# A graph layer: the rows of one tile in every second batch come from one-hot products on PE instead of a gather

## The reference

```
h   = max(layernorm(x), 0)
ea  = edge_attr @ W_edge.T + b_edge
msg = relu(h[src] + ea)
agg = segment_sum(msg, dst)
out = x + relu(((1 + eps) * h + agg) @ W1.T + b1) @ W2.T + b2
```

## Time and profile before

| | |
|---|---|
| time, median of 3 runs | 1233.08 us |
| time of the profiled execution | 1224.89 us |
| its span, first to last instruction | 1223.1 us |
| POOL busy | 785.8 us (64%) |
| DVE busy | 607.6 us (50%) |
| ACT busy | 518.7 us (42%) |
| PE busy | 496.0 us (41%) |
| mean granted TensorE clock | 0.673 |

### The profile page before, as it was taken

The page is one execution under the profiler, slowest core; times in us unless marked ns, Lnnn a source line. Parts: engine busy times, 40 slices in busy tenths (PEclk is TensorE's granted clock), DMA queues, the critical chain, the costliest instruction groups (busy, mean ns, idle before and its releaser), DMA issues.

```text
span 1223.1 us, 7306 instructions
## 1 busy us (share of the span) xinstructions
PE 496.0 (41%) x1592; PEld 249.7 (20%) x1592; DVE 607.6 (50%) x739; ACT 518.7 (42%) x713; POOL 785.8 (64%) x838
## 2 busy tenths in 40 slices
PE   2143344344344334245343253442534334425358
PEld 2011111222121112012111121120211111112146
DVE  6665544555554445364536345352545363543563
ACT  5134444344433335353435333343535343433434
POOL 6766666666666666575757575766757575757530
PEclk9967766767767766566666665666656666666669
DMA  7523333222223223242323332322423232322212
GB/s 217 148 66 71 83 78 68 67 68 68 67 67 68 68 68 98 56 112 71 81 71 80 72 79 64 72 68 61 101 54 82 63 72 64 71 64 67 47 28 79
DMA packets 51178, 93.18 MB, mean 76 GB/s; under 512 B 17722, under 2 KB 20443, under 8 KB 51136
## 3 DMA queue, kind: packets, MB, share of 16 engines
q0 software_dynamic: 26592, 40.85, 16.1%
q1 hardware_dynamic: 24390, 51.63, 15.6%
q10 hardware_dynamic: 154, 0.24, 0.1%
HBM read 87.85 MB, written 4.80 MB: 76 GB/s over the span
## 4 chain that ended last, share of the span: by engine, by line
another core or an unknown queue 32%; ACT 23%; issue 21%; DVE 13%; PE 6%; DVEq 4%; DMA 1%; SPq 0%; ACTq 0%
ACT edge_blocks L451 17%; ACT msg_parts L458 3%; DVE turn_ps L941 3%; DVE turn_ps L920 3%; PE turn_ps L505 2%; DVEq L834 2%; DVE turn_ps L926 2%; ACT msg_parts L463 2%; DVE msg_parts L955 1%; PE agg_ps L604 1%; PE turn_ps L667 1%; DVEq L836 1%; DVE stats L705 1%; DVE acc L825 1%
## 5 line engine op out<-in xcount | busy, mean ns | idle before, releaser
L375 POOL DMA_INDIRECT gathered<-h_table,src_all x810 | 764.4, 944 | 382.0 <-issue 237.7
L451 ACT COPY edge_blocks<-turn_ps 32x640 f32<-32x640 f32 (+1 forms) x480 | 325.9, 679 | 475.9 <-remote 358.8
L505 PE MATMUL turn_ps<-edge_in,w_edge 97*96 97x512 f32 x398 | 268.2, 842 | 324.2 <-issue 258.8
L926 DVE STREAM_TRANSPOSE turn_ps<-edge_blocks 128x960 f32<-128x960 f32 (+1 forms) x81 | 89.7, 1153 | 216.4 <-ACT edge_blocks L451 115.8
L853 DVE TENSOR_REDUCE sums<-agg_ps 128x192 f32<-128x576 f32 x41 | 30.9, 753 | 319.8 <-remote 319.8
L505 PEld LDWEIGHTS turn_ps<-edge_in,w_edge 97*96 97x96 f32 x398 | 88.6, 234 | 482.9 <-issue 482.9
L604 PE MATMUL agg_ps<-msg_parts,select 128*128 128x288 bf16 x816 | 155.6, 367 | 0.0
L458 ACT ACTIVATE msg_parts<-turn_ps 128x960 bf16<-128x960 f32 (+1 forms) x83 | 79.2, 957 | 157.2 <-DVE turn_ps L941 110.3
L771 DVE TENSOR_TENSOR select<-const_ps,dst_rel 128x2560 bf16<-128x2560 f32 (+1 forms) x43 | 120.8, 2812 | 33.2 <-issue 28.5
L604 PEld LDWEIGHTS agg_ps<-msg_parts,select 128*128 128x128 bf16 x816 | 103.4, 127 | 46.1
L941 DVE TENSOR_TENSOR turn_ps<-turn_ps,gathered 128x960 f32<-128x960 f32 (+1 forms) x83 | 91.1, 1144 | 2.1 <-DVE gathered L760 0.5
(11 more groups left out here) (77 smaller groups left out, 187.9 us busy)
## 6 DMA issues: line engine op xcount, KB each, us to landing
edge_in<-edge_t_dram SPq DMA_DIRECT2D x165, 240.0 KB
gathered<-h_table,src_all POOLq DMA_INDIRECT x810
x_all<-x_dram SPq DMA_DIRECT2D x5, 420.0 KB
h_all<-x_dram SPq DMA_DIRECT2D x10, 210.0 KB
out_dram<-h_all SPq DMA_DIRECT2D x10, 210.0 KB
h_table<-h_all SPq DMA_DIRECT2D x3, 420.0 KB
h_table<-h_all SPq DMA_DIRECT2D x1, 630.0 KB
dst_by_row<-dst_rows_dram SPq DMA_DIRECT2D x1, 480.0 KB, 4.1
```

The lines of the kernel that those rows point to most:

```text
L375: nc.gpsimd.indirect_dma_start(out=gathered[c % SLOTS][:, at:at + D], out_offset=None, in_=table, in_offset=bass.IndirectOffsetOnAxis(ap=s ...
L451: last = nc.scalar.copy(blocks[e:e + TURN, :, f:f + TURN], edges[f:f + TURN, :, e:e + TURN])
L505: mm = pe.matmul(turn_ps[0:D, q * BANK:q * BANK + (k1 - k0) * EDGE_TILE], w_edge[:], edge_in[c % SLOTS][:, k0 * EDGE_TILE:k1 * EDGE_TILE], ...
L926: last = nc.vector.transpose(in_flat(c, a, b), flat_rows(edge_blocks, a, b))
```

## The change

In the 11 even batches from 18 to 38 the last tile (tile 19) is no longer gathered. Its rows come from a table on the chip:

- In iterations 3 to 8 `h_all` is split, ten columns at a time, into three bf16 parts (`table_parts`): ACT copies the high and the middle part, DVE subtracts (`take_rest`, `take_low`).
- SP loads the 128 source numbers of the tile, the same for all 125 partitions, into `src_wide` (int32), behind a wait for an earlier compare.
- DVE compares them with the number of each of the 50 nodes that a partition holds (`make_hot(c)`, one instruction with an output of 125x6400 bf16, on the memory of `x_all`). The node numbers stand in PSUM, copied there once by ACT. It runs in iteration c-2, between the select and the transposes.
- PE multiplies: 50 matmuls of 125 rows, 128 columns of weights and 288 moved columns, summed in the bank `prep_ps` (`make_rows(c)`, in iteration c-1, behind the sums and ahead of the edge products; it waits for the compare and for ACT's moves of batch c-1, which read that bank).
- ACT copies the three parts to SBUF (iteration c-1, ahead of the moves), DVE sums them into the tile's place in `gathered` (`sum_rows`, iteration c-1, ahead of the transposes). The fifth edge product waits for ACT's copy, the adds of c wait for DVE's sum.
- The ones of `hidden` are written in iteration END instead of 16, since `x_all` is in use till then. The tail's edges are handled at iteration 16 instead of 18.

Line numbers in the rows of the changed program below are its own: L570 there is L505 before, L640 is L567, L677 is L604, L1032 is L926, L846 is L771, L947 is L872, L1049 is L941.

```diff
@@ constants
-HIDDEN_ONES_AT = 16
-TAIL_AT = 18
+TAIL_AT = 16
+PIECE_FROM = 3
+PIECE_COLS = 10
...
+    def one_hot(c):
+        return TAIL_AT + 2 <= c < END and c % 2 == 0
+    def one_hots_to(c):
+        return sum(one_hot(b) for b in range(c + 1))
+    def gathered_tiles(c, k0, k1):
+        return k1 - k0 - (one_hot(c) and k0 <= tiles_of[c] - 1 < k1)
...
@@ SP, iteration c
                 load_edges(c)
+                if c + 1 < BATCHES and one_hot(c + 1):
+                    b, tile = (c + 1) % 2, first_tile[c + 1] + tiles_of[c + 1] - 1
+                    if one_hot(c - 1):
+                        sp.wait_ge(hot_made, one_hots_to(c - 1))
+                    sp.dma_start(src_wide[b][:], src_rows[tile:tile + 1, :].broadcast_to((NP, EDGE_TILE))).then_inc(src_wide_in[b], 16)
@@ POOL
-                    for k in range(k0, k1):
+                    for k in range(k0, k0 + gathered_tiles(c, k0, k1)):
                         gather(h_table, c, k)
@@ ACT, iteration c, behind the splits of c and ahead of move_blocks(c + 1)
+                if 0 < c - PIECE_FROM <= PIECES:
+                    act.wait_ge(table_rest, c - PIECE_FROM)
+                    nc.scalar.copy(table_parts[:, piece(c - PIECE_FROM - 1), 1, :],
+                                   by_cols(x_all, c - PIECE_FROM - 1)).then_inc(table_middle, 1)
+                if 0 <= c - PIECE_FROM < PIECES:
+                    act.wait_ge(h_by_dve, DVE_PARTS)
+                    nc.scalar.copy(table_parts[:, piece(c - PIECE_FROM), 0, :],
+                                   by_cols(h_all, c - PIECE_FROM)).then_inc(table_high, 1)
+                if one_hot(c + 1):
+                    act.wait_ge(rows_done, one_hots_to(c + 1))
+                    if one_hots_to(c):
+                        act.wait_ge(rows_summed, one_hots_to(c))
+                    nc.scalar.copy(row_parts[:], rows_ps).then_inc(rows_moved, 1)
@@ PE, edge products, ahead of the fifth
+                        if one_hot(c):
+                            pe.wait_ge(rows_moved, one_hots_to(c))
...
+            def make_rows(c):
+                pe.wait_ge(table_low, PIECES)
+                pe.wait_ge(hot_made, one_hots_to(c))
+                pe.wait_ge(blocks_moved, c - 1)
+                for j in range(COLS):
+                    mm = pe.matmul(rows_ps, hot_rows[:, j, :], table_parts[:, j, :, :], start=(j == 0), stop=(j == COLS - 1))
+                mm.then_inc(rows_done, 1)
@@ PE, iteration c, behind the sums
+                if one_hot(c + 1):
+                    make_rows(c + 1)
@@ DVE
+            def take_rest(k):
+                dve.wait_ge(table_high, k + 1)
+                nc.vector.tensor_tensor(by_cols(x_all, k), by_cols(h_all, k), table_parts[:, piece(k), 0, :],
+                                        ALU.subtract).then_inc(table_rest, 1)
+            def take_low(k):
+                dve.wait_ge(table_middle, k + 1)
+                nc.vector.tensor_tensor(table_parts[:, piece(k), 2, :], by_cols(x_all, k), table_parts[:, piece(k), 1, :],
+                                        ALU.subtract).then_inc(table_low, 1)
+            def make_hot(c):
...
+                nc.vector.tensor_tensor(
+                    hot_rows, src_wide[c % 2][:].unsqueeze(1).broadcast_to((NP, COLS, EDGE_TILE)),
+                    ids_ps.unsqueeze(2).broadcast_to((NP, COLS, EDGE_TILE)), ALU.is_equal).then_inc(hot_made, 1)
+            def sum_rows(c):
...
+                nc.vector.tensor_reduce(gathered[c % SLOTS][:, tile * D:(tile + 1) * D],
+                                        row_parts[:].rearrange("p (k f) -> p f k", k=SPLIT), AX.X, ALU.add).then_inc(rows_summed, 1)
@@ DVE, add_rows
+                if one_hot(c):
+                    dve.wait_ge(rows_summed, one_hots_to(c))
@@ DVE, iteration c, behind the select and ahead of turn_blocks(c + 1)
-                if c == HIDDEN_ONES_AT:
-                    dve.wait_ge(h_by_act, ACT_PARTS)
-                    dve.wait_ge(h_by_dve, DVE_PARTS)
+                if 0 < c - PIECE_FROM <= PIECES:
+                    take_low(c - PIECE_FROM - 1)
+                if 0 <= c - PIECE_FROM < PIECES:
+                    take_rest(c - PIECE_FROM)
+                if one_hot(c + 1):
+                    sum_rows(c + 1)
+                if c + 2 < BATCHES and one_hot(c + 2):
+                    make_hot(c + 2)
+                if c == END:
+                    dve.wait_ge(rows_summed, one_hots_to(END))
                     nc.vector.memset(hidden[D:D + 1, :], 1.0).then_inc(hidden_ones_set, 1)
```

More of the change, by code:

```diff
@@ L59, in gnn_layer @@
 def gnn_layer(nc, x, edge_t, src_tiles, dst_tiles, dst_rows, w_edge_t, b_edge,
-              eps, w1_t, b1, w2_t, b2, out):
+              eps, w1_t, b1, w2_t, b2, src_rows, out):
     N, D = x.shape
@@ L1031 @@
         "b2": np.asarray(L0_gnn_b2),
+        "src_rows": by_tile(src).T,
     }
```

44 lines of the change are left out of this document (41 added, 3 removed).

## The result

The changed kernel takes 1288.46 us (1287.14 to 1291.13) and the kernel before, measured beside it, 1233.04 us (1232.31 to 1234.61): a ratio of 1.045 [1.043, 1.047], 4.5% slower. The forecast was 1221.2 us and "faster".

The account below looks back on a forecast made before the run. POOL's gathers were taken to bound the kernel from 92 to 1139 us; -15.5 (gathers) + 1.2 (table) + 2.4 (ones) = -11.9 us, giving 1221.2 us for the median, range 1216 to 1232.

Parts of the forecast that it names:

- Gathers removed: On POOL, one of 20 gathers less in each of 11 batches, at 1.4125 us each: 15.5 us less.
- The compare: DVE's one-hot compare between select and transposes: 6.85 us, 3.25 of them delaying the chain, a cost only beyond the room.
- rival C: DVE's compare takes 13.5 us and makes DVE's chain the bound: +16 to +82 and +3.6, some 1265 us; chance 0.07.
- Fifty matmuls on PE: Row products ahead of the edge products: 6.1 us all fast, 12.0 all slow, 7.8 mixed, ending at 706.7.
- covered, barely: Claim that the edge product behind the fifty, delayed by 3.25 us to 706.9, starts after they end at 706.7.
- I take 0: Pair's chain grows from 47.4 to 50 us or so, at worst 57.4, against POOL's 55.1: no cost counted.
- Room of 9.2 us per pair: The other engines finish a pair in 47.4 us and then stand, since POOL's pair takes 56.5 us.
- Table: Splitting the table in batches 3 to 8: ten DVE subtractions lengthen gathers by 0.12 us each, +1.2 us, bounds 0 to 6.
- Rival A: The table's subtractions on DVE block POOL for their whole length, +11.5 us: 1231.5 us, no change; chance 0.08.
- Ones at the end: DVE's 3.70 us memset, moved to iteration END ahead of the late selects: +2.4 us, bounds 0 and 3.7.
- Rival B: The 56.5 us period is not made by the gathers, so nothing is saved: +3.6, 1236.7 us, slower; chance 0.08.
- a gather of 1.41 us: POOL's time per gather: 1.25 us shown by the records, the rest paid in the pause when the run ends.

Follow-up runs that it names:

- e1: The kernel before with the 11 gathers (tile 19 of batches 18, 20, ... 38) left out and nothing in their place: 1216.25 us, ratio 0.989.
- e2: The changed kernel with one of the fifty row matmuls in each of the 11 batches, everything else kept: 1221.54 us, ratio 0.994.
- g1: The kernel before, POOL waiting ahead of the fourth gather of every group of five until the group before has landed: 1225.22 us, ratio 1.001.
- j1: The changed kernel with one POOL wait per one-hot batch, ahead of gather 9, for the first of the fifty row products: 1237.26 us, ratio 1.005.
- h3: The kernel before with two POOL waits for landed gathers in every second batch from 18 to 38: 1119.06 us, against 1081.63 on that chip.
- h1: The changed kernel with two POOL waits for landed gathers in each one-hot batch: 1111.0 us, where the kernel before takes 1081.63.
- e3: The kernel before, all gathers kept, with fifty unused 288-column matmuls ahead of the edge products of every second batch: 1292.29 us, ratio 1.051.
- f3: The kernel before with fifty unused matmuls of 32 columns instead of 288 ahead of every second batch's edge products: 1265.7 us, ratio 1.030.
- f4: The changed kernel with its fifty row products moved behind the fourth edge product, ahead of the fifth: 1467.77 us, ratio 1.183.
- e6: The kernel before without gathers from batch 2 on, plus fifty unused matmuls in each of the 11 even batches: 986.49 us, two executions.
- e5: The kernel before with no gather from batch 2 on, their rows missing: 1022.45 us, one execution.

## Why the prediction was wrong

*Gathers removed*: right. -15.5 was predicted, -14.1 measured in e1 (interval -15.9 to -11.8), pairs of 55.3 for 55.1.

*The compare*: 6.85 us predicted, 6.81 measured, and it costs nothing; rival C was rightly discounted.

*Fifty matmuls on PE: "covered, barely" and, for the chain, "I take 0"*. This is the step that failed. Its durations and its start were right for the first of the eleven rows: 11.7 us behind the release, at 0.16 us each. But it took for granted that PE goes on running while its signals are held. The prediction had written in its second paragraph that these signals come only when the run of gathers ends, and priced this at 2 us for the row copy. It did not ask how many instructions PE can have out behind a held signal. In the kernel before PE has 32 matmuls between the edge products in the first half of a pair and the next release (2 and 20 of the sums, 10 edge products), always just under the 35 to 37 at which it stops in the experiments. So no row of before shows the limit, and fifty more had to go over it. Where 0 was put, the cost was some 64 us: the changed kernel is 55.4 us above the one before on its chip, the same kernel with one of the fifty 8.8 us below (e2).

*Room of 9.2 us per pair*: it exists for work that waits for DVE or ACT, which get each other's signals at once. For fifty matmuls on PE it doesn't.

*Table*: +1.2 predicted, 0.4 measured. Some gathers are longer, up to 1.86 us in e2, but the run's end takes that up. Rival A (+11.5) is out: gathers are lengthened by some 4 us in all, and the time hardly moves.

*Ones at the end*: +2.4 predicted, 3.7 measured. DVE's 1.38 us of idle time did vanish, as said, but 0.97 us of new idle time came ahead of the memset and the select in front of it came 0.4 us late.

*Rival B* (the period is not made by the gathers): out, since leaving eleven out shortens it.

*The chances*: "slower" had been given 0.15, for rivals B and C. What came was slower, but by neither of them, so no rival of the prediction named it. And the upper end of the forecast, "about 1228", is 1229 by its own terms (1233.1 - 13.7 + 6 + 3.7).

What the prediction called a gather of 1.41 us is, more exactly, 1.25 us of POOL and 0.17 us of backlog, which any pause of POOL takes up and which one chip did not have at all.

What stays open: what the backlog is. It is not transfers yet to land (g1). It holds PE's completions, lets through one matmul with its weight load in 2.1 to 3.5 us while POOL gathers and for 2 to 5 us more, then one in 0.7 to 1.4 us, and does not touch ACT, DVE or the landings of gathers. What stops PE is open too: that its unfinished instructions fill a queue was argued from the count and not shown, and a PE that gets its next instructions late while the backlog lasts would look the same. Why one chip of six lacked it I can't say; each chip was used for one set of measurements, so the chip and its state at that time are not told apart.

## What to carry to other kernels

Where a profile shows an engine's signals held for tens of us (a wait ended by "remote", long after the producer's matmul), don't count its idle time there as cover, but count its instructions. Here it stopped after 35 to 37 matmuls with their weight loads, of 288 columns or of 32, where some thirty gathers had been issued, and after 63 where the run of gathers had only begun. A replacement that trades one instruction of the bounding engine for a hundred of an idle one is priced by their number first. Where such work must stand there, a wait of the gathering engine on the first instruction of that work lets the backlog clear when it is needed, and costs little where there is such a backlog, since it is taken off the pause at the end (j1). On the chip without one, two waits for landed gathers in every second batch from 18 to 38 cost 37 us (h3).

## What the runs showed of the hardware

- One kernel on six chips: 1224 to 1231 us on five, 1082 on one, 12% less. The profiles from that one chip (h1, h3) show no pause of POOL on "remote"; in the kernel before these make up 138.0 us, of the 143 between 1224.9 and 1081.6.
- The gaps between the single matmuls behind the stop are 0.7, 1.4, 2.1, 2.8 and 3.5 us to within 0.1: steps of 0.70 us, in the changed kernel, e3, f3 and f4 alike.
- Fifty matmuls that nobody needs can make a kernel faster: e6, with them, took 986.5 us and e5, without them, 1022.5 (one execution), on two chips where the kernel before takes 1224.3 and 1230.3. From 500 to 950 us the granted clock was 0.76 and 0.64. The edge products behind the fifty take 4.50 us, those behind an idle PE 6.96 to 7.46, and a pair takes 44.2 us instead of 47.5.
